# A two-layer graph attention kernel: x loaded in 4 KB pieces, layer 0 shifted by the top of one eighth, r of group 0 spread by a transfer

## The reference, cut to what matters

```python
# layer 0                       (layer 1 is alike, without L, THR and elu)
h = relu(layernorm(x)); h = h @ W
e = leaky_relu((h @ a_src)[:, None] + (h @ a_dst)[None, :], 0.2)
valid = (adj > 0) & (h.sum(axis=1) != 0)[None, :]
att = softmax(where(valid, e, -1e9), axis=1)
attention = where(att >= 1e-4, att, 0) * valid.sum(axis=1)[:, None]
x = x + elu(h + attention @ h)
```

## Time and profile before

| what | value |
|---|---|
| three timed runs | 1973.93, 1978.59, 1979.74 us; median 1978.59 |
| the profiled execution | 1969.02 us, its span 1967.1 us |
| TensorE clock granted, mean | 0.991 |
| PE busy | 1906.6 us (97%) |
| DVE busy | 1740.1 us (88%) |
| ACT busy | 1471.5 us (75%) |
| POOL busy | 1242.6 us (63%) |
| the chain that ended last | PE 86%, DMA 5%, DVE 4%, ACT 2% |

### The profile page before, as it was taken

One profiled execution on the slowest core, in us unless ns is written; L12 is line 12 of the kernel. 1 busy time (PEld: TensorE's weight loads), 2 busy tenths in 40 slices (PEclk: granted clock), 3 DMA queues, 4 the chain that ended last, 5 costly groups with the idle time before them and its releaser, 6 DMA issues.

```text
span 1967.1 us, 39089 instructions
## 1 busy us (share of the span) xinstructions
PE 1906.6 (97%) x16858; PEld 1898.0 (96%) x16858; DVE 1740.1 (88%) x2023; ACT 1471.5 (75%) x1745; POOL 1242.6 (63%) x1010
## 2 busy tenths in 40 slices
PE   4789999999999999999999999999999999999998
PEld 3689999999999999999999999999999999999997
DVE  7888898998989899898969898998989899898985
ACT  4988897888889888898771877777788777778710
POOL 3675776767767575775640777767677676768600
PEclk9799999999999999999999999999999999999999
DMA  8999898899989788897990798888989788888900
GB/s 252 349 344 342 291 320 268 299 328 344 319 287 334 275 304 285 309 328 268 370 361 12 262 365 290 299 306 292 338 285 332 274 300 308 293 329 295 329 19 13
DMA packets 181381, 566.46 MB, mean 288 GB/s; under 512 B 18768, under 2 KB 49872, under 8 KB 179664
## 3 DMA queue, kind: packets, MB, share of 16 engines
q0 software_dynamic: 142848, 520.16, 74.9%
q1 hardware_dynamic: 33424, 41.36, 6.3%
q10 hardware_dynamic: 4928, 2.36, 0.5%
HBM read 548.01 MB, written 15.79 MB: 287 GB/s over the span
## 4 chain that ended last, share of the span: by engine, by line
PE 86%; DMA 5%; DVE 4%; ACT 2%; POOL 1%; issue 1%; SPq 0%; DVEq 0%; POOLq 0%
PE psum L766 84%; DMA arena<-in_adj_dram,piece_rows 4%; ACT arena L360 2%; PE psum L724 1%; DVE arena L1063 1%; POOL arena L350 1%; DVE arena L864 1%; DVE arena L378 1%; DMA arena<-x_mid 1%; PE psum L713 0%; DVE st L839 0%; DMA arena<-in_x_dram 0%; POOL piece_rows L396 0%; PE psum L691 0%; DVE h_all L885 0%
## 5 line engine op out<-in xcount | busy, mean ns | idle before, releaser
L766 PE MATMUL psum<-h_all,arena 128*128 128x129 f32 x16384 | 1841.6, 275 | 10.1 <-DVE arena L1063 10.0
L766 PEld LDWEIGHTS psum<-h_all,arena 128*128 128x128 f32 x16384 | 1836.4, 192 | 13.0 <-DVE arena L1063 10.3
L350 POOL DMA_INDIRECT arena<-in_adj_dram,piece_rows x992 | 1233.2, 1243 | 623.7 <-ACT arena L360 434.0
L360 ACT ACTIVATE arena<-arena,half_step 128x1024 uint8<-128x1024 int32 x992 | 1370.5, 1440 | 287.2 <-DMA arena<-in_adj_dram,piece_rows 156.5
L1063 DVE SCALAR_TENSOR_TENSOR arena<-arena,sd_col 128x1024 f32<-128x1024 f32 x512 | 641.2, 1277 | 103.1 <-PE psum L766 98.4
L1063 DVE SCALAR_TENSOR_TENSOR arena<-arena,rho_col 128x1024 f32<-128x1024 f32 x448 | 563.5, 1278 | 69.3 <-PE psum L766 66.3
L378 DVE STREAM_TRANSPOSE arena<-arena 128x1024 f32<-128x1024 f32 x248 | 306.0, 1235 | 8.7 <-ACT arena L360 8.4
L360 ACT ACTIVATION_READ_ACCUMULATOR arena<-arena,half_step 128x1 f32 x512 | 92.5, 181 | 0.0
L1063 DVE SCALAR_TENSOR_TENSOR arena<-psum,rho_col,arena 128x1024 f32<-128x1024 f32 x64 | 79.1, 1267 | 6.8 <-PE psum L766 6.6
L724 PE MATMUL psum<-W_ext,arena 128*128 128x131 f32 x256 | 38.5, 313 | 13.5 <-DVE h_all L885 10.0
L724 PEld LDWEIGHTS psum<-W_ext,arena 128*128 128x128 f32 x256 | 36.3, 224 | 14.9 <-issue 10.6
(11 more groups left out here) (126 smaller groups left out, 195.1 us busy)
## 6 DMA issues: line engine op xcount, KB each, us to landing
arena<-in_adj_dram,piece_rows POOLq DMA_INDIRECT x992, 5.9
arena<-in_x_dram SPq DMA_DIRECT2D x48, 128.0 KB, 5.8
x_mid<-arena SPq DMA_DIRECT2D x8, 512.0 KB, 6.9
edgesT<-arena SPq DMA_DIRECT2D x4, 1024.0 KB, 9.1
arena<-edgesT SPq DMA_DIRECT2D x4, 1024.0 KB, 16.8
arena<-x_mid SPq DMA_DIRECT2D x8, 512.0 KB, 6.6
out_dram<-arena SPq DMA_DIRECT2D x28, 128.0 KB, 11.3
h_mid<-arena SPq DMA_DIRECT2D x6, 512.0 KB, 3.0
```

Of the source, the lines that this page charges most:

```text
L350: pool.indirect_dma_start(adj_in[n % NA], None, adj_pieces, bass.IndirectOffsetOnAxis(ap=piece_rows[:, column:column + 1], axis=0))\
L360: nc.scalar.activation(pack_bytes[h][:, k, a], adj_in[n % NA], ACT.Sign, bias=half_step[:, 0:1], accum_out=into).then_inc(masked, 1)
L766: last = nc.tensor.matmul(acc_tile(g, k), wTs[m % RING][:, k * P:(k + 1) * P], h_all[:, j, 0:FZ], start=(j == 0 and k % 2 == 0), stop=(j = ...
```

## The change

x is loaded in 16 transfers, not 32. Each partition of a block now takes eight neighbouring rows of x (4 KB in one piece) for each of two parts, where it took eight rows 32 apart (512 bytes each). So the rows lie in another order, and the copy of zT out of PSUM restores it: four instructions with 256 columns each, whose reads are 128 columns apart. There are four semaphores for x, one for a pair of parts. GpSimd still gathers three pieces once the first half of x is there, and the others once all is.

Layer 0's exponents are shifted by the top of part 0 (`find_reference(0, ...)`, three steps behind keep_h(0)), no longer by the top of all; the top of all and the lowest are found during group 0's steps and only checked against a limit (`judge`). r of group 0 is made by ACT ahead of piece 14 (`first_r`), limited and kept by DVE, turned by PE ahead of `products(0, 3)`, stored and loaded with broadcast (`load_r(4, ...)`); the diagonal is gone, and lin too. h of layer 0 lies densely in PSUM, which leaves room there for the turned rows.

```diff
@@ pool_fast
-            pool.wait_ge(x_loaded[XP // 2 - 1], 16 * BK)
+            pool.wait_ge(x_loaded[1], 16 * BK)
                 load_piece(pool, n)
                 if n == 2:
-                    pool.wait_ge(x_loaded[XP - 1], 16 * BK)
+                    pool.wait_ge(x_loaded[3], 16 * BK)
@@ load_x
-        def load_x(eng, i, which):
-            for q, block in quarters(x, i)[2 * which:2 * which + 2]:
-                eng.dma_start(x_all[q, part_of(0, i), :], block).then_inc(x_loaded[i], 16)
+        def load_x(eng, pair, which):
+            two = x_all[:, 2 * pair * TP:(2 * pair + 2) * TP, :].rearrange("p (i u) f -> p i (u f)", i=2)
+            for b in (2 * which, 2 * which + 1):
+                eng.dma_start(two[b * BP:(b + 1) * BP], eight_rows(pair, b)).then_inc(x_loaded[pair], 16)
@@ sync_fast
-            store_r(0, 0, T)
+            sp.wait_ge(z_turned[0], 1)
+            store_r(0, 0, G)
+            load_r(4, slice(0, GW))
+            store_r(1, G, T)
             load_r(0, slice(GW, 3 * GW))
             load_xr(0)
@@ scalar_fast
-                nc.scalar.activation(zTs[i % 2], zT_ps(0, i), ACT.Relu).then_inc(zT_ready[0], 1)
+                for b in range(BK):
+                    last = nc.scalar.activation(ordered_rows(zTs[i % 2], b), turned_rows(i, b), ACT.Relu)
+                last.then_inc(zT_ready[0], 1)
...
+            def first_r(t0, t1):
+                nc.scalar.activation(r_col[:, t0:t1], sd_col[:, t0:t1, 0], ACT.Exp, scale=ALPHA - 1.0,
+                                     bias=exp_bias[:, 1:2]).then_inc(r_ready, 1)
...
-                act.wait_ge(lin_ready, 1)
-                nc.scalar.activation(r_col[:], lin[:], ACT.Exp, scale=ALPHA - 1.0).then_inc(r_ready, 1)
+                act.wait_ge(first_sd_kept, 2)
                 nc.scalar.activation(D_col[:], d, ACT.Exp, scale=ALPHA, bias=exp_bias[:, 0:1])
                 nc.scalar.activation(rho_col[:], d, ACT.Exp, scale=1.0 - ALPHA, bias=exp_bias[:, 1:2])\
                     .then_inc(exps_ready, 1)
-                nc.scalar.activation(D_inv[:], d, ACT.Exp, scale=-ALPHA, bias=exp_bias[:, 2:3])
+                first_r(G, T)
+
+            def low_exps():
+                act.wait_ge(low_known, 1)
+                nc.scalar.activation(D_inv[:], sd_col[:, :, 1], ACT.Exp, scale=-ALPHA, bias=exp_bias[:, 2:3])
...
+                if i == FIRST_R:
+                    act.wait_ge(ref_ready, 1)
+                    first_r(0, G)
                 if i == PIECES - 2:
                     exps()
@@ tensor_fast
+                if i == 1:
+                    turn_extremes(0, first_spread_ps)
+                    spread_extremes(0, first_spread_ps)
+                    pe.wait_ge(ref_ready, 1)
+                if i == 3:
+                    turn_r(0, r_col, first_rT_ps, 0, G)
+                    pe.wait_ge(rows_ready, 1)
                 products(0, i)
-            turn_extremes(0)
-            spread_extremes(0)
-            spread_r()
@@ vector_fast
             keep_h(0)
+            for step in range(3):
+                find_reference(0, step)
+            normalise(0, 4, x_part(4), x_part(4))
             keep_h(1)
-            normalise(0, 4, x_part(4), x_part(4))
+            normalise(0, 5, x_part(5), x_part(5))
             keep_h(2)
-            normalise(0, 5, x_part(5), x_part(5))
-            keep_h(3)
+            limit_r(r_col, r_ready, 1, 0, G)
             dve.wait_ge(zT_ready[0], 4)
             keep_zT(4)
+            keep_rows(0, first_rT_ps, G)
             normalise(0, 6, x_part(6), x_part(6))
+            keep_h(3)
...
-            extreme_values()
-            diagonals()
+            dve.wait_ge(h_kept[0], 2 * XP)
+            keep_sd(G, T).then_inc(first_sd_kept, 2)
             dve.wait_ge(exps_ready, 1)
             fold(0)
             turn_edges(dve, 0, 1, 0)
-            dve.wait_ge(r_spread, 1)
+            dve.wait_ge(r_loaded[4], 16)
...
-                    if g == 0 and j == 0:
-                        keep_rows(0, rT_ps, T)
-                    if g == 0 and j == 2:
-                        judge(0)
+                    if g == 0 and j == 1:
+                        limit_r(r_col, r_ready, 2, G, T)
+                    if g == 0 and j == 8:
+                        keep_rows(1, rT_ps, T - G)
+                    if g == 0 and j == 9:
+                        first_extremes()
+                    if g == 0 and j == 15:
+                        reduce_extremes(1, spread_ps)
+                    if g == 0 and j == 21:
+                        keep_extremes(1).then_inc(low_known, 1)
+                        dve.wait_ge(low_known, 1)
+                        judge(0)
```

More of the change, by code:

```diff
@@ L70 @@
 RING = 4
+FIRST_R = 14
 FOLDS = 8
@@ L208, in kernel_program @@
         set_up = sem(p + "vector_set_up")
-        x_loaded = [sem(p + f"x_loaded{i}") for i in range(XP)]
+        x_loaded = [sem(p + f"x_loaded{i}") for i in range(XP // 2)]
         w_loaded = [sem(p + f"w_loaded{i}") for i in range(2)]
@@ L238, in kernel_program @@
         r_stored = sem(p + "r_stored")
-        r_loaded = [sem(p + f"r_loaded{i}") for i in range(4)]
+        r_loaded = [sem(p + f"r_loaded{i}") for i in range(5)]
         ref_ready = sem(p + "ref_ready")
@@ L333, in r_of @@
             row = g if layer == 0 else ORDER[g]
-            r = r_ps if layer == 0 and g == 0 else r_row[:, row * GW:(row + 1) * GW]
-            return r.rearrange("p (k n) -> p k n", k=BK)
+            return r_row[:, row * GW:(row + 1) * GW].rearrange("p (k n) -> p k n", k=BK)
         def piece(n):
@@ L637, in scalar_fast @@
             zT_at = {3: 0, 4: 1, 7: 2, 8: 3}
-            for i in range(XP):
-                load_x(act, i, 1)
+            for pair in range(XP // 2):
+                load_x(act, pair, 1)
             act.wait_ge(set_up, 1)
@@ L653, in scalar_fast @@
                 for i in range(PIECES):
+                    if s == COLS and i == 0:
+                        low_exps()
                     if s % COLS == 0 and i == 8:
@@ L879, in keep_zT @@
                     dve.wait_ge(h_done[0], 2 * (i - 1))
-                nc.vector.tensor_scalar(zTs[i % 2], zT_ps(0, i), 0.0, None, ALU.max).then_inc(zT_ready[0], 1)
+                for b in range(BK):
+                    last = nc.vector.tensor_scalar(ordered_rows(zTs[i % 2], b), turned_rows(i, b), 0.0, None, ALU.max)
+                last.then_inc(zT_ready[0], 1)
             def keep_h(i):
@@ new lines, in find_reference, with limit_r @@
+                    link(nc.vector.tensor_copy(ref[:], spread[:, P:P + 1]))
+                    if layer == 0:
+                        nc.vector.tensor_scalar(exp_bias[:, 2:3], ref[:], ALPHA, -SHIFT, ALU.mult, ALU.add)
+                    else:
+                        dve.wait_ge(low_ready, 1)
+                    shifts(ref).then_inc(ref_ready, 1)
+            def limit_r(source, sm, count, t0, t1):
+                dve.wait_ge(sm, count)
+                nc.vector.tensor_scalar(source[:, t0:t1], source[:, t0:t1], R_LIMIT, None, ALU.min).then_inc(r_limited, 1)
```

179 lines of the change are left out of this document (89 added, 90 removed).

## The result

The changed kernel takes 1992.6 us in the median of 8 runs (1987.57 to 1995.36), the kernel before 1977.43 beside it (1967.47 to 1979.74). The ratio is 1.0079, with an interval of 1.0061 to 1.0097: the medians differ by 15.2 us. The prediction was 1979.6, with 1985.5 as its upper end. The profiled execution after took 1994.54 us (span 1992.8).

A forecast was written before the change was run, and what follows sets the result against it. ACT's piece 63 was taken to set the end of the stretch. +2.6 us at piece 30 and -1.6 in the gathers gave +1.0, put on the median of 1978.59: 1979.6, range 1973 to 1985.5.

The forecast's parts named there:

- The gathers: Pieces 30 to 63 on ACT: loads of r and x mostly fall in the DMA hole during the iotas; -1.6 us.
- last sign of being wrong: A gather near 105 to 115 us over 3 us late, which would go to the end one for one.
- x: Load of x at the start: 4 KB pieces at about 380 GB/s bring DVE's chain 2.0 us earlier, keep_h(0) at 34.5.
- Rival (c): Load of x is no faster in 4 KB pieces: +3.4 us, 1982; sign: first statistics after 8.5; chance 0.10.
- bound of the first pair (8.9): Load of x: if 4 KB pieces are no faster, the first pair comes at 8.9 and DVE's chain 0.5 later.
- The reference: Behind keep_h(0): products(0,1) waits for the reference of one eighth and starts at 38.1 against 37.39, 0.7 us later.
- zT in four: Copies of zT out of PSUM in four: +0.65 us on ACT, +0.16 on DVE; a skill-based estimate gave +0.43 and +0.38.
- Rival (b): Reads of PSUM 128 columns apart run at half speed: +6.1 us at the end, 1984.7; chance 0.15.
- r of group 0: Ahead of ACT's piece 14: DVE loses 7.2 us at limit_r, PE about 9; products(0,3) starts near 54.6.
- Piece 30: On ACT, behind exps that wait for sd until 78.35: starts at 79.1 instead of 76.47, +2.6 us.
- The room at the sums: On PE: the start of the sums has 5.1 us of room; they begin at 84.6, +2.45, inside it.
- The median of before: Whole kernel: profiled execution took 1969.02, timed runs' median 1978.59, 9.6 more; the forecast +1.0 was put on that median.

The follow-up runs named there:

- Runs 1 and 2: before_r_sbuf and after_r_psum: r of group 0 in the other memory, in the kernel before and in the changed kernel; ratios 1.0022 and 1.0028.
- after_r_psum: Changed kernel with r of group 0 copied by DVE into free PSUM banks, where its tiles read it; ratio to the kernel before 1.0028.
- before_loads_gap: Kernel before with one more wait (13 tiles formed), so layer 1's r and x load in the gap between gathers; ratio 1.0013.
- before_r_sbuf: Kernel before with r of group 0 copied from PSUM to SBUF, where all its tiles read it; ratio 1.0022.

## Why the prediction was wrong, step by step

**The gathers (-1.6, in truth +7.8)** is the step that failed. It counted DMA traffic and put the effect of the tiles on the gathers at nothing, without a reason: it never asked where the tiles of group 0 would read r. The kernel's change shows it, since `r_of` drops its PSUM case, and the prediction costed the diagonal's removal and the transfer, but not the operand. Runs 1 and 2 put the price at 4.4 us in the old kernel and 10.1 in the new one. Without it the time would have come out inside the range (after_r_psum: 1.0028, about 1983). With r in PSUM, 30 to 63 takes the 54.9 us that were forecast (79.1 to 134.0). That is in part luck: in before_loads_gap the same move of the loads made the stretch 0.6 longer, not 1.6 shorter. The prediction's last sign of being wrong was a gather over 3 us late. Late gathers are what came, but for a reason that it did not have.

The Trainium skill has the rule, and it spoke against this change: "GPSIMD Engine Reference", section 1 on specifications, says that GpSimd's interfaces to SBUF are shared with VectorE, with contention from DVE instructions with two SBUF inputs. The trace agrees (0.94 us becomes up to 4.26, and the mean goes from 1304 back to 997 ns once r is in PSUM). The Trainium skill, "SBUF — State Buffer", section on who interferes with whom, makes the shared ports an exclusive lock. The end of the 3.21 us gather under the transpose of 124.59, which has one large operand, fits that; the gathers of 0.94 us beside the four tiles of before_r_sbuf do not.

**x (-2.0, in truth +1.7).** keep_h(0) starts at 38.26, not 36.54; 34.5 was forecast. The rate of 380 GB/s was borrowed from the gathers and is 287. And the first statistics now need a pair of parts, 1 MB and not 0.5 MB: 10.68 against 6.78. By the two rates the larger amount explains some 1.6 us of these 3.9 (an estimate: 1 MB at 287 against 0.5 MB at 259); the rest is open. Rival (c) was near the truth, x being a tenth faster only, and its bound of the first pair (8.9) was still too kind; its sign, first statistics after 8.5, came. The weights moved too, in the stretch to 24 us, before and then after (KB each, median us to landing):

```profile
W_ext<-in_L_gnn_W_dram SPq DMA_DIRECT2D x2, 64.0 KB, 4.7
a_three<-in_L_gnn_a_dram SPq DMA_DIRECT2D x4, 0.5 KB, 5.2
```

```profile
W_ext<-in_L_gnn_W_dram SPq DMA_DIRECT2D x2, 64.0 KB, 8.5
a_three<-in_L_gnn_a_dram SPq DMA_DIRECT2D x4, 0.5 KB, 9.6
```

They were issued at the same time as before (0.76 us) and landed almost 4 us later beside the larger pieces. On DVE the copies of the turned weights stand ahead of the statistics and come at 8.18 and 9.15 instead of 5.40 and 6.37. But the statistics still wait 1.37 us for x behind them, so x sets their start, and the weights cost nothing that a run shows.

**The reference (+0.7).** Behind keep_h(0) it took 3.9 us to products(0,1) (38.26 to 42.18), where 3.6 was forecast. Right in size; what should have paid for it was the error of x.

**zT in four (+0.65 on ACT, +0.16 on DVE).** ACT's four take 1.07 us from start to start, DVE's 1.33, against 0.92 and 1.14 for the one copy: +0.15 and +0.19. ACT's was put too high, and so was the estimate of +0.43 and +0.38. Rival (b) is wrong: at half speed a quarter was to cost 0.21 to 0.27 more, and all four together cost less than that.

**r of group 0 (DVE 7.2, PE about 9).** limit_r waited 7.12, PE's turn of r 7.29 and 1.14 behind it. The mechanism and the sizes are right; products(0,3) is 59.08 instead of 54.6 because its start had already slipped: piece 8 by 4.4.

**Piece 30 (+2.6, in truth +7.4 in this execution, +4.2 in after_r_psum).** The difference to 79.1 is 4.8 in after: 3.8 from x, 0.3 from the reference, 0.9 from PE's clock, less 0.5 for the cheaper quarters, carried through piece 14, and 0.3 behind it. The clock was missing from the sum: behind the longer idle spell PE has the 1.2 GHz level through the products of part 1 and into the transposes behind them, which take 1.79 us and not 1.06, so keep_first_zT(3) follows the start of these products by 5.48 instead of 4.60 us. The windows of after show it (columns as in the earlier trace rows):

```profile
42.00:46.00 4.00, 3.82 (x17) 3.82 (x18) 2.87 (x12) 0.00 (x0) 0.00 (x0) 0.50 0.32 117
46.00:50.00 4.00, 4.00 (x32) 4.00 (x31) 3.91 (x11) 2.34 (x5) 0.00 (x0) 0.83 0.03 6
```

In the kernel before, the stretch from 41 to 45 is granted 1.00. The exponentials waited 2.12 us for sd_col as foretold, to 83.10 and not 78.35. In after_r_psum, whose front is the same, they begin at 79.89 and piece 30 at 80.70, only 1.6 over the forecast: piece 8 is 3.2 later than forecast there (47.51), and the way from it to piece 30 is 1.6 shorter. So of the 4.8, 3.2 belong to this execution.

**The room at the sums (5.1).** It was read rightly and never used: the later sums (+7.4) still ran ahead of piece 63.

**The median of before.** The 9.6 us between its profiled execution and its median were carried over unchanged. The wait near 1020, absent there alone, is of that size (3.7 to 9.5). The carrying did little harm: the medians differ by 15.2 where step 26 moved by 15.3.

## What to carry to other kernels

Where GpSimd issues gathers, count how many operands of the large VectorE instructions beside them lie in SBUF. Moving one operand from PSUM to SBUF hardly changed the tiles' own time here (1272 against 1260 ns) and cost the kernel 0.2 to 0.5%. The trace of before could have told: the same instruction with both operands in SBUF ran in its later groups, and the gathers beside it were a third longer. When a transfer is re-cut, count what the first consumer must wait for before the rate: behind one semaphore for a pair of parts the statistics began 3.9 us later. And a rate borrowed from another kind of transfer (414 GB/s of gathers, where x got 287) is no measurement.
